# Ten small embedding tables looked up on TensorE: one-hot products in two float32r parts, against three bfloat16 parts

## What is computed

```python
e = stack([tbl_f[ids[:, f]] for f in range(26)], axis=1)     # 26 tables of 128 columns
all = concatenate([bottom[:, None, :], e], axis=1)           # [2048, 27, 128]
gram = einsum('bfd,bgd->bfg', all, all)                      # 27 x 27 for each sample
h = concatenate([gram[:, TRIU_I, TRIU_J], bottom], axis=1)   # 351 + 128 = 479 columns
h = maximum(h @ W_top1 + b_top1, 0)                          # 479 -> 512
h = maximum(h @ W_top2 + b_top2, 0)                          # 512 -> 256
y = h @ W_top3                                               # 256 -> 1
```

## Time and profile before

| | |
|---|---|
| median of 3 runs | 413.85 us |
| lowest, highest | 411.24, 420.0 us |
| the profiled execution: its time, its span | 416.7 us, 414.6 us |
| mean granted TensorE clock in it | 0.992 |
| gathers on POOL | 296 |
| products `hot_ps` on PE | 1560 |

### The profile page before, as it was taken

One profiled execution on the slowest core, in us unless ns is written; L12 is line 12 of the kernel. 1 busy time (PEld: TensorE's weight loads), 2 busy tenths in 40 slices (PEclk: granted clock), 3 DMA queues, 4 the chain that ended last, 5 costly groups with the idle time before them and its releaser, 6 DMA issues.

```text
span 414.6 us, 10787 instructions
## 1 busy us (share of the span) xinstructions
PE 377.4 (91%) x4368; PEld 327.4 (79%) x4368; DVE 214.6 (52%) x715; ACT 229.2 (55%) x444; POOL 294.7 (71%) x305
## 2 busy tenths in 40 slices
PE   0788849698999999999999999999999999999997
PEld 0567738587888788878888788878887888888886
DVE  6898886353634644356353643445434556324242
ACT  3555985544454565645535365656565363538851
POOL 6887777777777777777777777777777777777200
PEclk9999979999999999999999999999999999999999
DMA  5576672112222222322222223222322122122100
GB/s 181 147 247 206 174 263 86 53 53 84 54 57 57 52 54 84 90 53 78 59 53 59 56 55 84 59 58 53 84 84 59 53 53 52 51 57 53 28 1 2
DMA packets 15712, 33.00 MB, mean 80 GB/s; under 512 B 5680, under 2 KB 6448, under 8 KB 15408
## 3 DMA queue, kind: packets, MB, share of 16 engines
q0 software_dynamic: 9472, 19.42, 17.9%
q1 hardware_dynamic: 6192, 12.90, 9.7%
HBM read 32.29 MB, written 0.01 MB: 78 GB/s over the span
## 4 chain that ended last, share of the span: by engine, by line
PE 71%; POOL 18%; issue 6%; DVE 3%; DMA 1%; ACT 1%; ACTq 0%; DVEq 0%
PE hot_ps L321 31%; POOL X L278 18%; PE gram_ps L304 12%; PE h_ps L363 9%; PE zh_ps L376 7%; PE xt_ps L289 6%; PE h_ps L360 4%; DVE onehot L465 2%; PE zh_ps L343 1%; ACT gram_sb L442 1%; DMA X<-in_table_dram,rows_sb 1%; DVE h L503 1%; DMA rows_sb<-in_rows_dram 1%; PE hot_ps L363 0%; DVE Z L473 0%
## 5 line engine op out<-in xcount | busy, mean ns | idle before, releaser
L278 POOL DMA_INDIRECT X<-in_table_dram,rows_sb x296 | 293.4, 991 | 91.6 <-issue 88.7
L321 PE MATMUL hot_ps<-onehot,tab 128*128 128x256 bf16 x1560 | 184.0, 276 | 17.0 <-ACT tab L625 12.0
L321 PEld LDWEIGHTS hot_ps<-onehot,tab 128*128 128x128 bf16 x1560 | 153.9, 99 | 37.0 <-issue 14.5
L442 ACT COPY gram_sb<-gram_ps 32x208 f32<-32x208 f32 x254 | 129.6, 510 | 96.7 <-PE gram_ps L304 87.9
L465 DVE TENSOR_SCALAR onehot<-ids_wide,row_value 128x256 bf16<-128x256 int16 x520 | 109.9, 301 | 84.8 <-PE hot_ps L321 84.1
L304 PEld LDWEIGHTS gram_ps<-XT 128*64 128x64 f32 x2048 | 64.9, 138 | 13.7 <-issue 13.0
L304 PE MATMUL gram_ps<-XT 128*64 128x52 f32 x2048 | 73.1, 224 | 0.2 <-ACT XT L430 0.2
L590 ACT COPY XT<-hot_ps 128x256 f32<-128x256 f32 x60 | 36.7, 612 | 47.8 <-PE hot_ps L321 47.2
L289 PE MATMUL xt_ps<-ident,X 128*128 128x128 f32 x296 | 44.7, 278 | 12.0 <-DMA X<-in_table_dram,rows_sb 10.8
L289 PEld LDWEIGHTS xt_ps<-ident,X 128*128 128x128 f32 x296 | 35.1, 141 | 17.8 <-DMA X<-in_table_dram,rows_sb 11.5
L363 PE MATMUL h_ps<-stage_sb,w_sb 128*128 128x256 f32 (+3 forms) x198 | 45.1, 363 | 0.0
(11 more groups left out here) (41 smaller groups left out, 109.2 us busy)
## 6 DMA issues: line engine op xcount, KB each, us to landing
X<-in_table_dram,rows_sb POOLq DMA_INDIRECT x296
ids_wide<-in_hot_ids_dram SPq DMA_DIRECT2D x11, 320.0 KB, 3.6
stage_sb<-in_hot_dram SPq DMA_DIRECT2D x10, 320.0 KB, 3.9
stage_sb<-in_hot_dram SPq DMA_DIRECT2D x10, 256.0 KB, 3.2
bottomT<-in_bottom_t_dram SPq DMA_DIRECT2D x1, 1024.0 KB, 7.0
w_sb<-in_w_dram SPq DMA_DIRECT2D x1, 1024.0 KB, 9.6
w_sb<-in_w_dram SPq DMA_DIRECT2D x1, 512.0 KB, 11.3
ids_wide<-in_hot_ids_dram SPq DMA_DIRECT2D x5, 64.0 KB, 2.9
```

The source lines that it names most:

```text
L278: pool.indirect_dma_start(X[:, n % RING, k, :], None, table, bass.IndirectOffsetOnAxis(idx[:, column:column + 1], 0)).then_inc(gathered[n ...
L321: mm = pe.matmul(hot_ps[i % 2][:, 0:WIDE], tab[u][:, part, D * c:D * (c + 1)], onehot[i % 2][:, c, :], start=(c == 0 and part == 0), stop= ...
L442: kept = copy(gram_sb[rows, :, GROUPS_PER_BLOCK * j:GROUPS_PER_BLOCK * (j + 1)].rearrange("p n g -> p g n"), gram_ps[rows, b % 2, 0:GROUPS ...
```

## The change

The one-hots are float32r as well, and are kept in a ring of three pieces of at most four chunks in place of two whole tables: the 8-chunk tables have two pieces, the 10-chunk tables three. Six of the eight pairs now look up ten tables (`HOTS`), two look up six. So there are 100 products for a pair with six tables and 180 for one with ten, 1280 in all, 640 one-hots in place of 520, and 68 units or 272 gathers in place of 74 and 296. To make room, the ring `X` has 5 units, `bottomT` holds 6 tiles and is loaded in eight pieces, and the memory reserved for the descriptors of POOL's DMAs is set to 4096 bytes a partition, where before the default stood. The splits: one cast on ACT and one subtraction on DVE for each piece of a table.

```diff
-PARTS = 3
+PARTS = 2
-RING = 7
+RING = 5
-STAGES = 4
+STAGES = 5
+ONEHOTS = 3
+BOTTOMS = 6
+PIECE_MAX = 4
-HOTS = [HOT_BASE, HOT_BASE, HOT, HOT_BASE, HOT, HOT_BASE, HOT_BASE, HOT]
+HOTS = [HOT_BASE, HOT, HOT, HOT, HOT_BASE, HOT, HOT, HOT]
...
+def pieces(chunks):
+
+    count = -(-chunks // PIECE_MAX)
+    return [-(-chunks * h // count) for h in range(count + 1)]
...
-        tab = [sb(f"tab{u}", [ROWS, PARTS, HC[u] * D], bf16) for u in range(HOT)]
-        onehot = [sb(f"onehot{s}", [ROWS, HC_MAX, WIDE], bf16) for s in range(2)]
-        bottomT = sb("bottomT", [P, TILES, P])
+        tab = [sb(f"tab{u}", [ROWS, PARTS, HC[u] * D], fp32r) for u in range(HOT)]
+        onehot = [sb(f"onehot{s}", [ROWS, PIECE_MAX, WIDE], fp32r) for s in range(ONEHOTS)]
+        bottomT = sb("bottomT", [P, BOTTOMS, P])
...
                     if at == PRODUCTS[n][u]:
+                        wait(pe, hot_placed, i - 1)
+                    h = sum(1 for begin in PIECE[u][1:] if begin <= c)
+                    p = ASKED_AT[i, h]
+                    if part == 0 and c == PIECE[u][h]:
                         if n < 2:
-                            pe.wait_ge(part0, 2 * (u + 1))
-                            pe.wait_ge(part1, 2 * (u + 1))
-                            pe.wait_ge(part2, 2 * (u + 1))
-                        pe.wait_ge(onehot_ready, i + 1)
-                        wait(pe, hot_placed, i - 1)
-                    mm = pe.matmul(hot_ps[i % 2][:, 0:WIDE], tab[u][:, part, D * c:D * (c + 1)], onehot[i % 2][:, c, :],
+                            pe.wait_ge(part0, FIRST_PIECE[u] + h + 1)
+                            pe.wait_ge(part1, FIRST_PIECE[u] + h + 1)
+                        pe.wait_ge(onehot_ready, p + 1)
+                    mm = pe.matmul(hot_ps[i % 2][:, 0:WIDE], tab[u][:, part, D * c:D * (c + 1)],
+                                   onehot[p % ONEHOTS][:, c - PIECE[u][h], :],
                                    start=(c == 0 and part == 0), stop=(c == HC[u] - 1 and part == PARTS - 1))
                     if at + 1 == PRODUCTS[n][u + 1]:
                         mm.then_inc(hot_full, 1)
+                    elif part == PARTS - 1 and c + 1 == PIECE[u][h + 1]:
+                        mm.then_inc(piece_used, 1)
...
-                wait(dve, hot_full, i - 1)
-                for c in range(HC[u]):
-                    compared = dve.tensor_scalar(onehot[i % 2][:, c, :], ids_wide[:, u, :], row_value[:, c:c + 1], None,
-                                                 ALU.is_equal)
+                before = p - ONEHOTS
+                if before >= 0 and is_last(before):
+                    dve.wait_ge(hot_full, ASKED[before][0] + 1)
+                elif before >= 0:
+                    dve.wait_ge(piece_used, sum(1 for k in range(before + 1) if not is_last(k)))
+                for c in range(PIECE[u][h], PIECE[u][h + 1]):
+                    compared = dve.tensor_scalar(onehot[p % ONEHOTS][:, c - PIECE[u][h], :], ids_wide[:, u, :],
+                                                 row_value[:, c:c + 1], None, ALU.is_equal)
...
-                dve.tensor_tensor(part, part, tab[u][:, 0, at], ALU.subtract).then_inc(rest, 1)
...
-                dve.tensor_tensor(tab[u][:, 2, at], stage[q % STAGES][:, 0:at.stop - at.start], tab[u][:, 1, at],
-                                  ALU.subtract).then_inc(part2, 1)
+                dve.tensor_tensor(tab[u][:, 1, at], stage[q % STAGES][:, 0:at.stop - at.start], tab[u][:, 0, at],
+                                  ALU.subtract).then_inc(part1, 1)
...
-    nc = _bacc.Bacc("TRN2", target_bir_lowering=False, num_devices=1)
+    nc = _bacc.Bacc("TRN2", target_bir_lowering=False, num_devices=1, dynamic_dma_scratch_size=4096)
```

More of the change, by code:

```diff
@@ L87, in build @@
 def build(nc, table, rows_in, hot_ids, hot_tables, bottom_t, w1, b1, w2, row_vecs, out):
-    fp32, bf16, i16, i32 = mybir.dt.float32, mybir.dt.bfloat16, mybir.dt.int16, mybir.dt.int32
+    fp32, fp32r, i16, i32 = mybir.dt.float32, mybir.dt.float32r, mybir.dt.int16, mybir.dt.int32
     ALU = mybir.AluOpType
@@ L93, in build @@
     HC_MAX = max(HC)
-    PIECE = [(0, c // 2, c) for c in HC]
-    PIECE_MAX = max(max(b - a, c - b) for a, b, c in PIECE)
+    PIECE = [pieces(c) for c in HC]
+    FIRST_PIECE = [sum(len(p) - 1 for p in PIECE[:u]) for u in range(HOT + 1)]
+    PIECE_OF = [(u, h) for u in range(HOT) for h in range(len(PIECE[u]) - 1)]
+    ASKED = [(i, u, h) for i, (n, u) in enumerate(LOOKUPS) for h in range(len(PIECE[u]) - 1)]
+    ASKED_AT = {(i, h): p for p, (i, u, h) in enumerate(ASKED)}
     PRODUCTS = [[PARTS * sum(HC[:u]) for u in range(h + 1)] for h in HOTS]
@@ L147, in build @@
         stage_in = [sem(f"stage_in{s}") for s in range(STAGES)]
-        bottom_in = sem("bottom_in")
+        bottom_in = [sem(f"bottom_in{s}") for s in range(BOTTOMS // 2)]
         w1_in = sem("w1_in")
@@ L221, in load_high_ids @@
             def load_high_ids(n):
-                wait(sp, onehot_ready, FIRST[n])
+                wait(sp, onehot_ready, ASKED_AT[FIRST[n], 0])
                 sp.dma_start(ids_wide[:, LOW:HOTS[n], :],
@@ L228, in load_piece, with load_bottom @@
             def load_piece(q):
-                u, h = q // 2, q % 2
+                u, h = PIECE_OF[q]
                 begin, end = PIECE[u][h], PIECE[u][h + 1]
-                wait(sp, part2, q - STAGES + 1)
+                wait(sp, part1, q - STAGES + 1)
                 sp.dma_start(stage[q % STAGES][:, 0:D * (end - begin)], hot_tables[u][:, D * begin:D * end]
                              ).then_inc(stage_in[q % STAGES], 16)
+            def load_bottom(k):
+                slot = k % (BOTTOMS // 2)
+                if k >= BOTTOMS // 2:
+                    sp.wait_ge(h1_full, C1 * (k - BOTTOMS // 2 + 1))
+                    sp.wait_ge(bottom_placed, 2 * (k - BOTTOMS // 2 + 1))
+                sp.dma_start(bottomT[:, 2 * slot:2 * slot + 2, :], bottom_t[:, 2 * k:2 * k + 2, :]
+                             ).then_inc(bottom_in[slot], 16)
             sp.dma_start(rows_sb[:], rows_in).then_inc(rows_loaded, 16)
@@ L241, in _ @@
             load_high_ids(0)
-            for q in range(STAGES, 2 * HOT_BASE):
+            for q in range(STAGES, FIRST_PIECE[HOT_BASE]):
                 load_piece(q)
             sp.dma_start(b1_sb[:], b1).then_inc(b1_in, 16)
-            sp.dma_start(bottomT[:], bottom_t).then_inc(bottom_in, 16)
+            load_bottom(0)
             load_low_ids(1)
-            for q in range(2 * HOT_BASE, 2 * HOT):
+            for q in range(FIRST_PIECE[HOT_BASE], FIRST_PIECE[HOT_BASE + 1]):
                 load_piece(q)
             load_high_ids(1)
+            for q in range(FIRST_PIECE[HOT_BASE + 1], FIRST_PIECE[HOT]):
+                load_piece(q)
+            load_bottom(1)
+            load_bottom(2)
             sp.dma_start(w1_sb[:], w1).then_inc(w1_in, 16)
@@ L536, in step @@
                     u = HOT_BASE + b
-                    split_rest(2 * u)
-                    split_rest(2 * u + 1)
-                    split_last(2 * u)
-                    split_last(2 * u + 1)
+                    for q in range(FIRST_PIECE[u], FIRST_PIECE[u + 1]):
+                        split_second(q)
                 if t >= 3 and t % 2 == 1 and j == 3:
@@ L654, in step @@
                     relu(len(JOBS) - 2, 2 * (j - 2) + 1)
-            split_first(0)
-            for q in range(2 * HOT_BASE):
-                if q + 1 < 2 * HOT_BASE:
-                    split_first(q + 1)
-                split_second(q)
-                if q % 2 == 1 and q > 2:
-                    place_hot(q // 2 - 1)
+            for u in range(HOT_BASE):
+                for q in range(FIRST_PIECE[u], FIRST_PIECE[u + 1]):
+                    split_first(q)
+                if u > 0:
+                    place_hot(u - 1)
             moves(0)
             place_hot(HOT_BASE - 1)
-            act.wait_ge(bottom_in, 16)
             act.wait_ge(b1_in, 16)
```

96 lines of the change are left out of this document (46 added, 50 removed).

## The result

The changed kernel takes 398.91 us (median of four runs, 398.03 to 401.86) against 415.11 for the kernel before, run beside it: a ratio of 0.965, 95% interval 0.955 to 0.975. It is faster, by 16 us; the forecast was 379, which is 36 less. The direction was right and the size was not. The profiled execution has a span of 396.4 us (before: 414.6).

The account below looks back on a forecast made before the run. Gathers were taken to bound the first 101 us and PE the rest; 91 us to block 11's gram plus 288 behind it gave 379 us, own range 371 to 388 (60%), wider range 370 to 412.

Parts of the forecast that it names:

- The first stretch: From the start to the gram of block 11: bound by gathers, 91 us, 14.4 earlier than 105.4.
- Rival A, two cycles a column: TensorE's float32r products take 0.216 us each, two cycles a column, giving some 490 us; chance 15%.
- The product at 0.112: Each float32r product on TensorE costs 0.112 us, one pass of its 256 columns.
- second stretch: From the gram of block 11 to the end: 288.0 us in place of 309.2, with products giving -21.0.
- One-hots at 0.195 "at nothing": 640 one-hots on DVE at 0.195 us, 125 us in place of 101, adding nothing to the span; DVE near 60%.
- Rival B: Four-byte one-hots take 0.33 us, PE waits some 0.3 us in each of 44 slices: 392 us (388 to 400); chance 10%.
- Behind pieces of four it is less (-2.5): PE's 5.3 us wait for DVE's layer 3 shrinks by 2.5; the same amount returns as waits at the ring.
- Rival C, one-hots hold up gathers: Each one-hot delays gathers by 0.34 us, adding 43 to their 374: 417 us, POOL the bound; chance 12%, mostly at half price.
- a tie with the gathers at block 36: Block 36's gather lands at 217 us and PE arrives at 218, so 1.5 us is added.

Follow-up runs that it names:

- bf16_onehots_b: Changed kernel, but from the second pair one-hots are written as bf16 into tiles no product reads; products read old float32r ones: 385.35 us, ratio 0.926.
- prices: A separate kernel timing series of matmuls of one form each, and 24 one-hots of each form alone and beside 40 gathers; float32r product 0.120 us, one-hot 0.263.
- narrow_products_c: Changed kernel with layer 3 ahead of the one-hots, and from the second pair each product moving only 128 of 256 columns: 386.61 us, ratio 0.928.
- tables_as_before: Changed kernel with the earlier kernel's choice of looked-up tables: 296 gathers, 1040 products; 402.89 us, ratio 0.969, where the kernel before takes 416.8.
- few_onehots: Changed kernel, but from the second pair only the first one-hot of each piece is made: 491.47 us on a slow chip, 379.33 us (ratio 0.912) repeated elsewhere.
- few_gathers: Changed kernel, but from the sixteenth unit only one of a unit's four gathers is made: 425.44 us on a slow chip, 393.43 us (ratio 0.946) repeated elsewhere.

## Where the prediction failed, and what of it was right

The forecast of 379 us missed 398.91 by 20. The step that failed is the cost of the one-hots, which it kept at 0.195 us and added at nothing: they took 0.304, and what stands behind them on VectorE came late. A second term, the product at 0.112 us, was too small by 0.008.

- **The first stretch: its length right, its bound not, and some luck in it.** The forecast added up 30 us to the gram of block 0, 51 of TensorE's own work and 10 of waits for gathers. Measured: 35.0, since the prelude's 50 one-hots take 0.26 to 0.31 us and not 0.195; then 52.4 of work and 4.5 of waits, none of them for a gather. Gathers were sized too slow as well: the 60th began at 80.4 and not 83.4. They still stand close behind VectorE, as `bf16_onehots_b` shows, which gains 3.8 us at block 0 and has 0.7 of them left at block 11.
- **Rival A, two cycles a column: refuted.** 256 columns of float32r in 0.120 us are 1.1 cycles each at 2.4 GHz. The Trainium skill (SBUF — State Buffer, A bandwidth-pool intuition that's wrong) puts TensorE's moving operand at 2 bytes a lane, by which a 4-byte operand would take two cycles a column. The rows of `prices` don't bear that out for float32r.
- **The product at 0.112: a term too small.** It was taken from float32 records of 128 columns, and with 128 columns a float32r product does take 0.112; with 256 it takes 0.120. 910 products by 0.008 are 7.3 us of TensorE. Taking them out (`narrow_products_c`) shortens the second stretch by 4.4, since one-hots are then in the way for 3.7.
- **One-hots at 0.195 "at nothing", with "DVE stays near 60%": the step that failed.** 0.263 for the output type, 0.304 with gathers beside them, and DVE at 72%. Rival B had the type's price as a possibility, too high at 0.33, and mis-stated its place: TensorE hardly waits for one-hots in a slice (0.8 us behind 92 us). They delay something else that stands behind them on DVE.
- **"Behind pieces of four it is less (-2.5)": right for one-hots at the old price, and undone by the new one.** With bf16 one-hots in the same pieces the wait for layer 3 is 3.1 us, where 5.3 - 2.5 = 2.8 was forecast. With float32r ones it rose to 9.2 and took the clock with it twice. At the place shown above 15 one-hots stand in one run of 4.73 us ahead of layer 3; at a like place in the kernel before it was eight in 1.78:

```profile
274.72 1.78 DVE L465 TENSOR_SCALAR onehot<-ids_wide,row_value 128x256 bf16<-128x256 int16 x8 [1.39 <-PE hot_ps L321]
```

- **Rival C, one-hots hold up gathers: refuted for float32r output.** A gather is 962 ns on average (991 before), and it is the gathers that lengthen the one-hots. For float32 output see the end.
- **The sum.** In the second stretch TensorE is busy 10.8 us longer than forecast: 7.3 for the products' price and 3.3 for the clock, which falls twice. It is idle 5.7 longer, for the wait for layer 3. The runs give the same: 304.5; with layer 3 ahead 292.6 (-11.9); with the product at its forecast price too 288.2 (-4.4), where the forecast was 288.0. The time of 379 is still not reached: with both edits the span is 383.7, since that run's first stretch takes 95.5 us. The 1.5 us for a tie with the gathers at block 36 was not needed, as TensorE waits for none.
- **What float32r and what the tables bring.** float32r alone, with gathers as before, is at 0.969; the whole change at 0.965 (0.955 to 0.975). So as it stands, looking up more tables brings nothing that can be told apart. With layer 3 ahead the whole change is worth 0.932; what the same edit does with the tables as before was not run.

## What to carry to other kernels

When an edit makes one engine's operations longer or more, don't ask whether that engine stays below 100%, but what stands behind them in its program and who waits for that: here an engine at 72% cost 12 us through one small operation, and putting that first gave them back. Price an operation of a new type by its own rows, with its own width; a spacing from a narrower shape hid 7%. And where two engines are close to their bounds, an estimate that frees one is capped by the other: `tables_as_before` freed TensorE and waited for gathers for 24 us.

## What was not expected of the hardware

**A gather holds up a one-hot with float32r output, and these don't hold up gathers.** In `prices` the undelayed one-hots are 0.263 us apart beside gathers too, but one in each gather's time (they begin 1.25 us apart) takes up to 551 ns. The row of that line (least, middle and longest duration, first and last start), and that of 15 one-hots of the changed kernel:

```profile
L100 DVE TENSOR_SCALAR hot_r<-ids,value x24: 333/344/551, 99.0 to 105.7; 128x256 fp32r<-128x256 int16 x24
```

```profile
L518 DVE TENSOR_SCALAR onehot<-ids_wide,row_value x15: 333/343/547, 252.1 to 256.5; 128x256 fp32r<-128x256 int16 x15
```

The gathers keep their 0.94 us in both. With another output type it was the reverse, once. A gather of `prices` began shortly before the 24 one-hots with float32 output:

```profile
110.35 7.08 POOL L53 DMA_INDIRECT X<-in_table_dram,idx  x1 [0.30 <-issue]
110.92 6.38 DVE L110 TENSOR_SCALAR hot_f<-ids,value 128x256 f32<-128x256 int16 x24
```

It took 7.08 us and ended 0.13 behind the last of them, and they stayed 0.263 us apart and 0.336 long, as if it weren't there. That is one event, on a chip whose engines pause, though VectorE did not pause in it, and no run repeats it. But it means that which of the two gives way can't be told from the float32r rows for another type. The subtractions of the kernel before lengthened a gather too, to 2.30 us.

**Chips differ more than these kernels do.** On some the kernel before took 524 to 539 us and not 417. `few_onehots` took 491 us on such a chip and 379 elsewhere. A gather took 958 ns there and 963 elsewhere, a copy of the gram 519 and 517, a product 300 and 292 (granted clock 0.92 and 0.99). What differs most are pauses for which the trace names no work. TensorE's come to some 50 us, most of them ahead of products:

```profile
PE hot_ps L367 <- issue: 40.7, 41, 9.1
```

With 113 gathers in place of 272 the same chip gave 425 (`few_gathers`), so the gathers have a part in it; how, and what makes up the rest of the difference, stays open. A ratio measured on such a chip doesn't carry over: `tables_as_before` stood at 0.988 and 0.995 there, at 0.969 on the other.
